# Roots of the query and key norms moved to VectorE, a later second weight split, and stack fetches in front of the low parts' store

## The reference

```python
qkv = (x1 @ mat_qkv_w.T + qkv_bias).reshape(B, L, 3, H, hd)
q, k, v = [jnp.transpose(qkv[:, :, i], (0, 2, 1, 3)) for i in range(3)]
q = _l2norm(q) * sm            # x / sqrt(sum x^2), times a scale for each head
k = _l2norm(k)
scores = jnp.einsum('bhqd,bhkd->bhqk', q, k)
probs = jax.nn.softmax(scores, axis=-1)
...
x = x + attn_out * gamma1
x2 = _ln(x) * (scale2 + 1.0) + shift2
h = jax.nn.gelu(x2 @ fc1_w.T + fc1_b, approximate=False)
x = x + (h @ fc2_w.T + fc2_b) * gamma2
```

## Time and profile before

| | |
|---|---|
| median of three runs | 837.64 us |
| profiled execution | 836.95 us, of which the span is 835.2 us |
| mean granted TensorE clock | 0.979 of full speed |
| busy in the span | TensorE 766.2, VectorE 491.3, ScalarE 477.6, GpSimd 380.8 us |
| graph layer, about 0 to 260 us | TensorE nearly always busy |
| attention, about 275 to 634 us | one turn every 21.1 us |
| FFN, about 634 us to the end | TensorE nearly always busy |

### The profile page before, as it was taken

One profiled execution on the slowest core, in us unless ns is written; L12 is line 12 of the kernel. 1 busy time (PEld: TensorE's weight loads), 2 busy tenths in 40 slices (PEclk: granted clock), 3 DMA queues, 4 the chain that ended last, 5 costly groups with the idle time before them and its releaser, 6 DMA issues.

```text
span 835.2 us, 15488 instructions
## 1 busy us (share of the span) xinstructions
PE 766.2 (92%) x4964; PEld 561.5 (67%) x4964; DVE 491.3 (59%) x1010; ACT 477.6 (57%) x765; POOL 380.8 (46%) x638
## 2 busy tenths in 40 slices
PE   4989999999997589999999999999868999999997
PEld 3878778787875345666666666666545888888885
DVE  1378888888887555666666665565453443444433
ACT  1334444444444357777777777777745655555553
POOL 0157575757575655555555555554560212222110
PEclk9989999999999789999999999999979999999999
DMA  8701212131300666566666666666710000000001
GB/s 246 245 23 48 94 48 93 47 93 47 93 13 13 115 114 114 115 111 113 113 115 109 107 112 115 114 110 112 118 20 1 0 26 26 26 26 14 26 24 40
DMA packets 68604, 65.59 MB, mean 79 GB/s; under 512 B 10832, under 2 KB 67792, under 8 KB 68560
## 3 DMA queue, kind: packets, MB, share of 16 engines
q1 hardware_dynamic: 67232, 64.87, 36.6%
q10 hardware_dynamic: 1328, 0.16, 0.1%
HBM read 48.09 MB, written 16.78 MB: 78 GB/s over the span
## 4 chain that ended last, share of the span: by engine, by line
PE 64%; ACT 11%; DVE 10%; issue 7%; POOL 2%; DMA 1%; SPq 1%; ACTq 0%; DVEq 0%; POOLq 0%
PE ps L1567 10%; PE ps L1581 10%; PE ps L1293 6%; PE ps L1457 5%; PE ps L1443 5%; ACT probsT L820 4%; PE ps L1495 3%; PE ps L1395 3%; PE ps L1334 3%; PE ps L1269 2%; PE ps L1284 2%; PE ps L1323 2%; PE ps L1476 2%; ACT w_ada L849 2%; ACT weightT L757 1%
## 5 line engine op out<-in xcount | busy, mean ns | idle before, releaser
L820 ACT ACTIVATE probsT<-ps 128x1024 f32<-128x1024 f32 x128 | 130.9, 1023 | 48.7 <-PE ps L1443 48.7
L1191 DVE TENSOR_TENSOR hidden_low<-hidden,hidden_high 128x512 fp32r<-128x512 f32 x64 | 46.6, 728 | 107.2 <-ACT hidden_high L931 59.2
L1097 DVE TENSOR_REDUCE neg_max<-ps 128x4 bf16<-128x344 f32 x128 | 64.2, 512 | 56.7 <-PE ps L1410 55.9
L1443 PE MATMUL ps<-q_stack,k_stack 97*128 97x256 bf16 x512 | 79.5, 278 | 10.4 <-ACT probsT L820 6.2
L1443 PEld LDWEIGHTS ps<-q_stack,k_stack 97*128 97x128 bf16 x512 | 43.1, 98 | 67.0 <-ACT probsT L820 30.4
L928 ACT ACTIVATE hidden<-ps,b_fc 128x512 f32<-128x512 f32 x64 | 44.1, 689 | 69.6 <-PE ps L1567 69.6
L1457 PE MATMUL ps<-probsT,v_ones 128*32 128x256 f32 x1024 | 68.5, 385 | 9.2 <-ACT probsT L820 9.1
L608 POOL TENSOR_TENSOR scores<-scores,row_max 128x640 f32<-128x640 f32 x32 | 40.8, 1276 | 76.6 <-DVE row_max L966 76.6
L1387 PE MATMUL ps<-w_qkv,x1T 128*128 128x512 f32 x128 | 64.8, 631 | 2.8 <-DVE rest L1104 2.8
L1293 PE MATMUL ps<-x_res,w_q 128*128 (+1 forms) x256 | 62.9, 390 | 0.0
L1293 PEld LDWEIGHTS ps<-x_res,w_q 128*128 128x128 f32 x256 | 46.8, 192 | 10.8 <-issue 5.5
(11 more groups left out here) (173 smaller groups left out, 1893.2 us busy)
## 6 DMA issues: line engine op xcount, KB each, us to landing
parts_dram<-w_ada SPq DMA_DIRECT2D x96, 128.0 KB
q_stack<-parts_dram SPq DMA_DIRECT2D x96, 128.0 KB, 4.3
adj<-in_adj SPq DMA_DIRECT2D x16, 440.0 KB, 4.2
k_stack<-parts_dram SPq DMA_DIRECT2D x16, 384.0 KB, 7.7
xT<-in_xT SPq DMA_DIRECT2D x16, 256.0 KB, 3.0
x_in<-in_x SPq DMA_DIRECT2D x16, 256.0 KB, 2.7
k_stack<-parts_dram SPq DMA_DIRECT2D x16, 256.0 KB, 8.6
out_x<-result SPq DMA_DIRECT2D x16, 256.0 KB, 2.1
```

The lines of the kernel that those rows point to most:

```text
L820: nc.scalar.activation(probsT[:, s % 4, :], ps[:, COLS:COLS + 2, :].rearrange("p a n -> p (a n)"), ACT.Exp).then_inc(exp_made, 1)
L1097: nc.vector.tensor_reduce(places[:, :, k], ps[:, ROW_BANKS[n % 2], 0:4 * KP].rearrange("p (a g) -> p a g", a=4), AX_X, ALU.max, negate=Tru ...
L1191: nc.vector.tensor_tensor(hidden_parts[1][:, s % H_SLOTS, :], hidden[:, s % RAW, :], hidden_parts[0][:, s % H_SLOTS, :], ALU.subtract).the ...
L1443: mm = nc.tensor.matmul(ps[:, COLS + j, kt * N:(kt + 1) * N], k_stack[:, par, place, kt * P:(kt + 1) * P], q_stack[:, par, place, :], star ...
```

## The change

Four things move. The three Newton steps go from GpSimd to VectorE, with the addition of 1.5 and the last product in one instruction: nine instructions for twelve, and one for the head scale. They stand in slot 3, behind the row maximum of that slot and in front of `divide`; in the part written by hand they stand behind `take_output(B - 2)`. SyncE fetches the eight blocks of high and middle rows as soon as the four high and middle stores have landed, in front of the store of the low parts, and the two low blocks behind it: ten DMAs for nine, with as many bytes. In the transition to the FFN, GpSimd splits w_fc1 before it makes the norm roots and w_fc2 only when VectorE has made the parts of pair 0; ScalarE lays the scaling of pair 0 between the first exponentials of turn 17; and the first two FFN steps move to slots 4 and 6. Behind the turns, the fourth FFN step comes ahead of the first `second`.

```diff
-    FIRST_AT = (2, 4)
+    FIRST_AT = (4, 6)
...
+        def get_high_and_mid(n, par):
+            sp.wait_ge(parts_out, 4 * 16 * (n + 1))
             ge(sp, st_mm, n * 8 - 8)
-            for slot, part in enumerate(Q_PARTS):
-                sp.dma_start(rows(q_stack, slot, 1), whole(0, part, 1)).then_inc(stack_in, 16)
-            for slot, n in ((0, 3), (3, 2), (5, 1)):
-                sp.dma_start(rows(k_stack, slot, n), whole(1, 0, n)).then_inc(stack_in, 16)
+            for slot in range(NSLOT - 1):
+                sp.dma_start(rows(q_stack, par, slot, 1), whole(0, Q_PARTS[slot], 1)).then_inc(stack_in, 16)
+            for slot, m in ((0, 2), (3, 2), (5, 1)):
+                sp.dma_start(rows(k_stack, par, slot, m), whole(1, 0, m)).then_inc(stack_in, 16)
+
+        def get_low(n, par):
+            sp.wait_ge(low_out, 2 * 16 * (n + 1))
+            sp.dma_start(rows(q_stack, par, NSLOT - 1, 1), whole(0, 2, 1)).then_inc(stack_in, 16)
+            sp.dma_start(rows(k_stack, par, 2, 1), whole(1, 2, 1)).then_inc(stack_in, 16)
...
             if b is not None:
+                get_high_and_mid(b, 1 - par)
                 put_part(b, 1 - par, 2, low_made)
-                get_stacks(b, 1 - par)
+                get_low(b, 1 - par)
...
             if f is not None:
-                roots(f)
                 blocks_of_pairs(f, par)
...
                 pool.wait_ge(g["late_weights"], g["LATE"])
-                ffn_root(0)
                 split(w_fc1, w1_high, w1_low, w1_split)
+                ffn_root(0)
             if isinstance(c, int) and c == B - 1:
...
+                pool.wait_ge(x2_low, C2)
                 split(w_fc2, w2_high, w2_low, w2_split)
...
-                    ffn_scale(0)
                 if c is not None and s < 8:
                     probabilities(c, s)
+                if isinstance(c, int) and c == B - 1 and s < C2:
+                    ffn_scale(0, (s,))
...
+        def newton(f, n):
+            old, new = root[(n + 1) % 2], root[n % 2]
+            if n:
+                dve.wait_ge(root_step, f * ROOT + 4 * n)
+            nc.vector.tensor_tensor(root_sq[:], old[:], old[:], ALU.mult).then_inc(root_step, 1)
+            dve.wait_ge(root_step, f * ROOT + 4 * n + 1)
+            nc.vector.tensor_tensor(root_err[:], root_sq[:], minus_half[:], ALU.mult).then_inc(root_step, 1)
+            dve.wait_ge(root_step, f * ROOT + 4 * n + 2)
+            nc.vector.scalar_tensor_tensor(out=new[:], in0=root_err[:], scalar=1.5, in1=old[:], op0=ALU.add, op1=ALU.mult
+                                           ).then_inc(root_step, 2)
...
+                if f is not None and s == 3:
+                    roots(f)
                 if d is not None and s == 3:
                     divide(d)
...
         for s in range(LEAD, STEPS + LAG):
-            if s < STEPS:
+            if s < STEPS and s != LEAD + 1:
                 first(s)
-            if s == 2:
+            if s == LEAD:
                 output_tokens(B - 1, None, COLS)
+                first(LEAD + 1)
```

More of the change, by code:

```diff
@@ L229, in _ @@
                                             base=0, pattern=[[-HD, HT]], channel_multiplier=1).then_inc(chain, 1)
-                    pool.wait_ge(chain, 5)
+                    pool.wait_ge(chain, 4)
                     nc.gpsimd.affine_select(out=head_of_row[:], in_=head_of_row[:], compare_op=ALU.is_ge, fill=0.0,
@@ L554, in put_part, with rows, whole @@
                 sp.wait_ge(made, 2 * n + w + 1)
-                sp.dma_start(parts_dram[w, :, part], parts[:, par, w, part]).then_inc(parts_out, 16)
-        def get_stacks(n, par):
-            sp.wait_ge(parts_out, 6 * 16 * (n + 1))
-            ge(sp, st_mm, n * 8 - 8)
[L561 to L565, removed]
-            for slot, part in enumerate(Q_PARTS):
-                sp.dma_start(rows(q_stack, slot, 1), whole(0, part, 1)).then_inc(stack_in, 16)
-            for slot, n in ((0, 3), (3, 2), (5, 1)):
-                sp.dma_start(rows(k_stack, slot, n), whole(1, 0, n)).then_inc(stack_in, 16)
+                sp.dma_start(parts_dram[w, :, part], parts[:, par, w, part]).then_inc(low_out if part == 2 else parts_out, 16)
+        def rows(stack, par, at, n):
+            return stack[at * SLOT:(at + n) * SLOT, par].rearrange("p (h c) n -> p h (c n)", c=C2)
+        def whole(w, part, n):
+            return parts_dram[w, :, part:part + n].rearrange("h a d x -> (a d) h x")
+        def get_high_and_mid(n, par):
+            sp.wait_ge(parts_out, 4 * 16 * (n + 1))
+            ge(sp, st_mm, n * 8 - 8)
+            for slot in range(NSLOT - 1):
[6 more added lines that the diff above has]
+            sp.dma_start(rows(k_stack, par, 2, 1), whole(1, 2, 1)).then_inc(stack_in, 16)
         def turn(f, b, c, d, par):
@@ L639, in _ @@
         turns(graph_turn, pool, 3)
[L642 to L660, removed]
-            nc.gpsimd.tensor_tensor(by[:, :, 0, :], by[:, :, 0, :], head_scale[:].unsqueeze(1).broadcast_to([P, T, H]),
-                                    ALU.mult).then_inc(root_step, 1)
         def low_part(f, par, w):
@@ L694, in turn @@
                 pool.wait_ge(g["late_weights"], g["LATE"])
+                split(w_fc1, w1_high, w1_low, w1_split)
                 ffn_root(0)
-                split(w_fc1, w1_high, w1_low, w1_split)
             if isinstance(c, int) and c == B - 1:
-                pool.wait_ge(parts_out, 6 * 16 * B)
+                pool.wait_ge(parts_out, 4 * 16 * B)
                 pool.wait_ge(s_mm, GROUPS * B)
+                pool.wait_ge(x2_low, C2)
                 split(w_fc2, w2_high, w2_low, w2_split)
@@ L720, in _ @@
         normalise(B - 1, 1, 1)
-        roots(0)
         pool.wait_ge(x_made, B)
@@ L885, in turn, with ffn_scale @@
                 take_sums(c, 1)
-        def ffn_scale(n):
+        def ffn_scale(n, channels=range(C2)):
             act.wait_ge(xt_mm_f, n + 1)
             ge(act, x2_low, C2 * n)
-            for k in range(C2):
+            for k in channels:
                 for h in range(2):
@@ L1083, in first_guess, with roots @@
             nc.vector.tensor_scalar(root[1][:].bitcast(I32), root[0][:].bitcast(I32), -1.0, SEED, ALU.mult, ALU.add).then_inc(seeded, 1)
+        def newton(f, n):
[8 more added lines that the diff above has]
+                                           ).then_inc(root_step, 2)
+        def roots(f):
+            dve.wait_ge(seeded, 4 * (f + 1))
+            for n in range(3):
+                newton(f, n)
+            dve.wait_ge(root_step, f * ROOT + 12)
+            by = root[0][:].rearrange("p (t w h) -> p t w h", t=T, w=2)
+            nc.vector.tensor_tensor(by[:, :, 0, :], by[:, :, 0, :], head_scale[:].unsqueeze(1).broadcast_to([P, T, H]),
+                                    ALU.mult).then_inc(root_step, 1)
         def unit_qk(f):
@@ L1219, in _ @@
         take_output(B - 2)
+        roots(0)
         graph_residual(B - 2, 0)
```

19 lines of the change are left out of this document (9 added, 10 removed).

## The result

| | before | changed |
|---|---|---|
| median | 837.66 us (4 runs, 834.9 to 839.46) | 848.59 us (4 runs, 847.77 to 850.12) |
| profiled execution | 836.95 us | 849.12 us |
| its span, mean granted clock | 835.2 us, 0.979 | 847.4 us, 0.985 |
| busy TensorE, VectorE, ScalarE, GpSimd | 766.2, 491.3, 477.6, 380.8 us | 767.7, 516.9, 478.8, 315.1 us |

The ratio is 1.0127, with a 95% interval of 1.0104 to 1.0151: slower by 10.9 us, twice what was forecast, and just outside the range. The mean clock was no lower than before, so a lower clock over the whole run is not the reason.

A forecast was written before the change was run, and what follows sets the result against it. TensorE was taken to bound the kernel, carrying 64% of the chain of waits. Terms +11.6 - 2.0 - 4.2 = +5.4 us on 836.95 gave 842.35, 843.0 on the median; stated 842.5 us, range 837 to 848.

The forecast's parts named there:

- Roots in the turns: Turns 3 to 15: Newton steps on VectorE before `divide` delay o_tok, 0.84 us a turn, 1.5 in turn 15; +11.6 us.
- a wait at L1493: Sign of being right: TensorE waits 0.7 to 1.1 us for VectorE there in each turn from 3 on.
- upper bound: Roots in the turns: all nine instructions at 255 ns plus 0.05, 1.45 us for a turn, 19 us.
- First passage: Turn 0 to scores of turn 2: earlier roots and stack fetches, scores at 291.9 instead of 293.89; -2.0 us.
- The sign at 292 for the scores: Sign of being right: scores of turn 2 start near 292.
- Passage to the FFN: Turns 16 to 17: earlier normalisations 2.3, shorter chain 3.3, less 1.4 for a moved FFN step; gain 4.2 us.
- (1): Rival: chained roots before the division are hidden, nine in under 1.3 us; 830.7 us; chance 0.10.
- (2): Rival: a draw, both passages at their best and roots at the short end, 9 us; 836.6 to 839; chance 0.20.
- (3): Rival: stacks arrive late, TensorE waits about 0.9 us more in fourteen turns; 855 us; chance 0.07.
- (4): Rival: splitting w_fc1 slows VectorE's reductions in turn 16, at most 2.3 us; 844.8; chance 0.08.

## Why the prediction was right in kind and short in size

**Roots in the turns: the term that failed.** The mechanism was right (a wait at L1493, in each turn from 3 on, nothing given back), the size was not. It stood at 0.84 us for a turn; the two lengths of a turn, 44.94 us together against 42.19, make 1.37. Of the missing 0.53, 0.39 is the nine instructions: 2.54 us against 2.15. I had taken 0.19 for a fused instruction, under the mean of its larger form in the earlier trace rows, and let it start 0.03 behind its producer; it takes 0.22 to 0.23 and starts 0.10 behind. Another 0.04 is a later start of L1117 in every second turn (0.47 or 0.38 behind the reciprocal). The last 0.1 I can't put down to one instruction. Turn 15 was 22.20 us long, 1.95 over before, where 1.5 was forecast. With turn 3 (+1.5) the term is 18.5 us for 11.6. The upper bound given for it, 19 us, held; the value was chosen too near the short end. The range for the time didn't take that bound in: with 19 us the prediction's own sum is 849.8 us, over the 848 where the range ended.

**First passage.** Forecast -2.0, measured -1.91. The chain counted was the right one: the scores waited for a DMA at its end, and the low parts' store, for which the prediction took the 6.19 us of the earlier trace rows as its sign, took 6.20. Its 0.9 us for the low stores' data took writes as faster than fetches, for which no row stands; no run shows that term by itself. That neither edit would give the gain alone was not said. The sign at 292 for the scores came at 290.21 because the graph layer ended 1.77 us earlier in that execution.

**Passage to the FFN.** Forecast -4.2, measured -3.8. The four normalisations, against the earlier trace rows, with TensorE behind them:

```profile
622.98 1.37 DVE L1183 TENSOR_SCALAR x_hat_f<-x_res,mean_var_f,rstd_f 128x256 f32<-128x256 f32 x4
```
```profile
624.41 1.09 PE L1557 MATMUL ps<-ident,x_hat_f 128*128 128x128 f32 x8 [1.22 <-DVE x_hat_f L1183]
...
631.49 1.91 PE L1481 MATMUL ps<-ident,o_sumsT 128*128 128x128 f32 x8
...
653.34 0.66 PE L1493 MATMUL ps<-ident,o_tok 128*128 128x128 f32 x4 [1.06 <-DVE o_tok L1117]
```

L1557 to L1481 take 7.08 us (told 7.2, 10.5 in the earlier trace rows). The wait for the normalised values shrank from 3.53 to 1.22 us, the 2.3 forecast. The FFN step moved behind them opened the 1.06 us wait at the last o_tok. Turn 15 to 16 took 1.0 us more, with a lower clock:

```profile
606.00:612.00 6.00, 5.03 (x25) 3.86 (x23) 1.09 (x3) 2.69 (x4) 5.84 (x7) 0.72 0.78 118
```

In all fourteen traces this stretch goes by that: 18.65 to 19.15 us in the five in which the clock stays up in it, 20.16 to 20.35 in the nine in which it falls. The kernel with the fetch order alone has the fall; those with the roots in slot 4 and with the unfused steps, which keep everything else of the change, don't. So no edit decides it as far as one trace of each can tell.

**Rivals.** (1) fell: the chain is slower than forecast, not free. (2) fell with it. (3) fell: no wait for stacks in the middle turns, and none in the turns without the roots. (4) fell: from o_tok's transposes in turn 16 to the last piece ahead of L1557 TensorE took 8.59 us, as before, and the four normalisations took 1.37.

**The sum.** 18.5 - 1.9 - 3.8 + 1.0 + 0.15 - 1.77 = 12.2 us of span. Against 5.4 forecast, 6.9 come from the one term. That the rest adds up to about nothing is luck: +1.0 and -1.77 go with the clock in two other places, and the early end of the graph layer hides part of the cost. The direction was right by its mechanism.

## What to carry to other kernels

A chain of small dependent instructions is priced by its waits for the one before, and what it costs is set by the place: in front of what the bounding engine waits for, all of it counts that is longer than the idle time that was there, in gaps of VectorE's own list nothing; look for the gaps (here 1.04 and 1.92 us) and cut the chain to fit them. Price an unseen form by its slowest near relative when it stands on the path and is paid in every turn. Where two edits work on two chains that meet, neither has a worth of its own: try them together before dropping one.

## What the runs showed of the hardware

- A fused addition and product (128x64, fp32) starts 0.10 us behind its producer's end, a plain product or scalar operation 0.03. That is so in the loop (456.22 to 456.32 us) and in the part written out by hand (264.39 to 264.49). Why is open.
- On VectorE two independent halves of 32 columns take 0.22 us together, one instruction of 64 columns 0.25 to 0.33 in a chain; a free one starts 0.11 us behind the start of the one in front.
- Behind three of five waits of 1.73 us TensorE's clock fell to 1.2 GHz for some 3.7 us, which cost 1.4 us each time. Behind waits of 1.06, 1.25 and 1.54 us in the turns it never fell, nor behind single ones of 1.74 and 2.22 us.
- The graph layer, the same code in all kernels, ended between 262.35 and 267.57 us, and how often the clock fell to its lower level in the first 62 us goes with it: not at all in the two traces with 262.35 us, twice in the ten with 264.12 to 266.01, three times in the two with 267.47 and 267.57. The changed kernel was traced with none and with two falls, so it is not the edits. Its first 100 us in the two traces, columns as in the earlier trace rows:

```profile
0.00:100.00 100.00, 83.17 (x476) 67.78 (x476) 59.16 (x120) 34.85 (x63) 42.83 (x74) 1.00 0.44 134
0.00:100.00 100.00, 84.46 (x465) 68.61 (x466) 58.27 (x118) 32.93 (x60) 42.79 (x74) 0.97 0.41 128
```

  A single trace can't tell a change under 5 us unless it is cut at such events.
